# Sparse weights times rows as seven block products per pair of chunks

## What is computed

```python
inter = xf @ c1_w.T @ c2_w.T                      # scores, 1792 per row
blk = inter.reshape(B * T, n_blocks, SPARSITY)    # 56 blocks of 32
idx = argmax(blk, axis=-1) + arange(0, 1792, 32)  # one winner a block
h = relu(einsum('bkm,bm->bk', w1[idx], xf))
out = einsum('bk,bkm->bm', h, w2t[idx])
x = layernorm(x + out)
```

## Time and profile before

| what | us |
|---|---|
| median of three runs (733.7 to 734.46) | 734.05 |
| profiled execution, its span | 731.9 |
| TensorE busy in it | 722.7 |
| VectorE busy | 480.2 |
| ScalarE busy | 214.3 |
| GpSimd busy | 157.1 |

### The profile page before, as it was taken

One profiled execution on the slowest core, in us unless ns is written; L12 is line 12 of the kernel. 1 busy time (PEld: TensorE's weight loads), 2 busy tenths in 40 slices (PEclk: granted clock), 3 DMA queues, 4 the chain that ended last, 5 costly groups with the idle time before them and its releaser, 6 DMA issues.

```text
span 731.9 us, 8884 instructions
## 1 busy us (share of the span) xinstructions
PE 722.7 (99%) x3457; PEld 334.0 (46%) x3457; DVE 480.2 (66%) x930; ACT 214.3 (29%) x341; POOL 157.1 (21%) x131
## 2 busy tenths in 40 slices
PE   8999999999999999999999999999999999999996
PEld 3444444444444444444444444444444444445444
DVE  5978897796877779677767779653755361125136
ACT  1575457435612212122122112122212221122130
POOL 0452443111111111111111111222212212222130
PEclk9999999999999999999999999999999999999999
DMA  9537319310000010100001334104020015001001
GB/s 326 248 124 206 58 15 379 67 48 11 1 17 18 20 20 9 25 20 20 5 19 20 79 81 92 23 4 101 16 75 7 1 29 133 1 0 58 1 1 57
DMA packets 40569, 44.57 MB, mean 61 GB/s; under 512 B 25040, under 2 KB 32848, under 8 KB 39632
## 3 DMA queue, kind: packets, MB, share of 16 engines
q1 hardware_dynamic: 37552, 39.29, 17.9%
q0 software_dynamic: 2112, 4.19, 3.4%
q10 hardware_dynamic: 864, 0.53, 0.2%
HBM read 34.33 MB, written 4.42 MB: 53 GB/s over the span
## 4 chain that ended last, share of the span: by engine, by line
PE 86%; issue 1%; POOL 1%; DVE 0%; ACT 0%
PE acc L469 31%; PE pb L449 24%; PE pa L449 24%; PE acc L775 2%; PE acc L546 2%; PE pick_b L612 1%; PE pick_a L612 1%; POOL big L998 1%; PE pick_a L597 0%; PE pick_b L775 0%; PE acc L465 0%; PE pick_b L465 0%; ACT work L836 0%; ACT work L820 0%; ACT pick_b L821 0%
## 5 line engine op out<-in xcount | busy, mean ns | idle before, releaser
L469 PE MATMUL acc<-big,work 128*128 128x512 f16 x1038 | 234.3, 379 | 0.0
L991 POOL TENSOR_TENSOR work<-work 128x512 f16<-128x512 f32 x92 | 110.2, 1201 | 479.9 <-ACT work L909 270.0
L449 PE MATMUL pa<-xs,big 128*128 128x512 f16 x816 | 188.8, 379 | 0.0
L449 PE MATMUL pb<-xs,big 128*128 128x512 f16 x816 | 187.2, 379 | 0.0
L469 PEld LDWEIGHTS acc<-big,work 128*128 128x128 f16 x1038 | 101.5, 98 | 121.0
L449 PEld LDWEIGHTS pa<-xs,big 128*128 128x128 f16 x816 | 78.6, 98 | 91.8
L449 PEld LDWEIGHTS pb<-xs,big 128*128 128x128 f16 x816 | 78.5, 98 | 91.6
L964 ACT ACTIVATE work<-work 128x512 f16<-128x512 f32 x52 | 32.6, 627 | 203.1 <-DVE work L1611 203.1
L546 PE MATMUL acc<-big 128*128 128x512 f16 x336 | 73.9, 379 | 0.3 <-DVE big L1228 0.2
L1611 DVE SCALAR_TENSOR_TENSOR work<-big,const_sb,pa 128x512 f32<-128x512 f16 x28 | 20.8, 744 | 74.0 <-PE pa L449 67.4
L909 ACT ACTIVATE work<-work 128x512 f16<-128x512 f32 x40 | 25.2, 630 | 143.8 <-DVE work L1365 143.8
(11 more groups left out here) (176 smaller groups left out, 548.8 us busy)
## 6 DMA issues: line engine op xcount, KB each, us to landing
big<-in_w_all SPq DMA_DIRECT2D x2, 3840.0 KB, 17.2
big<-spread_rows SPq DMA_DIRECT2D x16, 448.0 KB, 9.1
big<-in_x_t SPq DMA_DIRECT2D x16, 256.0 KB, 8.7
rows<-in_x POOLq DMA_DIRECT2D x4, 1024.0 KB, 11.8
big<-in_w_all SPq DMA_DIRECT2D x2, 1536.0 KB, 11.2
out<-rows SPq DMA_DIRECT2D x3, 1024.0 KB, 4.3
big<-in_w_all SPq DMA_DIRECT2D x1, 2048.0 KB, 14.4
big<-in_w_all SPq DMA_DIRECT2D x2, 1024.0 KB, 11.6
```

Source lines behind the costliest of these rows:

```text
L449: mm = nc.tensor.matmul(dst[:, :], weights(wp)(kc * P, P), x_part16(g, xp, kc), start=(kc == 0 and wp == xp), stop=(kc == KC - 1 and wp == 1))
L469: mm = nc.tensor.matmul(acc[t][:, :], act_part(pair, j, ap, t * P, P), weights(wp)(0, H), start=(first and ap == wp), stop=(last and ap == 1))
L991: nc.gpsimd.tensor_tensor(act_part(pair, j, 1), act32[j], act_part(pair, j, 0), ALU.subtract).then_inc(act_lo, 1)
```

## The change

For each pair of chunks the hidden product (256 columns of weights by 512 rows, inner length 512) is cut in 2 x 2 blocks, and the eight block products are replaced by seven of sums of blocks (Strassen's identity in the form with shared sums). A block is 128 weight columns by 256 rows with inner length 256: 2 slices x 3 matmuls of 256 columns.

- `raise_quad` on GpSimd makes four sums in float32 (`quad`, 1024 columns) from two high-low pairs, `sums_high` on ScalarE makes the high part of them, `lower_quad` on GpSimd the low part. There are 15 such jobs: one for each of the seven units' weights, two for each group's rows. Five run in phase 1 (pairs 11, 12, 17, 18, 19), ten in the sparse phase, in the units 0 to 5, 8, 9, 15 and 16.
- `seven_products` on TensorE writes P1, then P5 and P7, then P2 and P6 (on P1), then P3 and P4, in halves of `pa` and `pb`. ScalarE copies P1, P5 and P7, and P1 + P6 to SBUF (`take_products`). VectorE adds two parts, of 256 and 512 columns, in `mask_hidden`, GpSimd two of 256 columns in `add_products`. The mask then reads `act32` instead of the PSUM banks.
- Spread loads go out in two parts for each group, 8 and 6 chunks.
- The order of the last second products is changed, one exponent of the scales is lower (`TOP2`), and the scratch for dynamic DMAs is 4096 bytes instead of the default.

```diff
+SUM_JOBS = (("w", 0), ("w", 1), ("x", 0, 0), ("x", 0, 1), ("w", 2), ("w", 3), ("w", 4), ("w", 5), ("w", 6),
+            ("x", 1, 0), ("x", 1, 1), ("x", 2, 0), ("x", 2, 1), ("x", 3, 0), ("x", 3, 1))
+JOB_IN_SWIGLU = {11: 0, 12: 1, 17: 2, 18: 3, 19: 4}
+JOB_IN_SPARSE = {0: 5, 1: 6, 2: 7, 3: 8, 4: 9, 5: 10, 8: 11, 9: 12, 15: 13, 16: 14}
...
+            def block_product(dst, weights, moving, first=False):
+                for k in range(KH):
+                    for wp, xp in ((0, 0), (0, 1), (1, 0)):
+                        mm = nc.tensor.matmul(dst, weights(k, wp), moving(k, xp), start=(first and k == 0 and wp == xp), ...
+            def seven_products(g, u, between=None, after_first=None):
...
+                if n:
+                    pe.wait_ge(c11_ready, n)
+                block_product(pa[:, low_half], w_block(0, 0), x_block(0, 0), True).then_inc(p1_ready, 1)
+                if n:
+                    pe.wait_ge(c12_ready, n)
+                else:
+                    pe.wait_ge(swiglu_ready, N1)
+                if u == 0:
+                    pe.wait_ge(sums_lo, SUM_JOBS.index(("x", g, 1)) + 1)
+                if g == 0:
+                    pe.wait_ge(sums_lo, SUM_JOBS.index(("w", u)) + 1)
+                block_product(pb[:, low_half], w_sum(SLOT_S1), x_sum(SLOT_T1), True)
+                block_product(pb[:, high_half], w_sum(SLOT_S3), x_sum(SLOT_T3)).then_inc(p57_ready, 1)
...
+                pe.wait_ge(p1_taken, n + 1)
+                block_product(pa[:, high_half], w_block(0, 1), x_block(1, 0))
+                block_product(pa[:, low_half], w_sum(SLOT_S2), x_sum(SLOT_T2)).then_inc(p26_ready, 1)
...
+                pe.wait_ge(p57_taken, n + 1)
+                block_product(pb[:, low_half], w_sum(SLOT_S4), x_block(1, 1))
+                block_product(pb[:, high_half], w_block(1, 1), x_sum(SLOT_T4)).then_inc(p34_ready, 1)
...
+            unit2(3, 4, none, none, none, "none")
+            for t in range(2):
+                second_tile(3, t, acc[t][:, :])
+            unit2(3, 5, none, none, none, "none")
+            second_tile(3, 2, acc[2][:, :])
+            for h, bank in enumerate(last_halves):
+                second_tile(3, TPG - 1, bank, h * HALF, HALF)
+            unit2(3, 6, none, none, none, "none")
+            for t in range(2):
+                for u in (4, 5):
+                    second_tile(u, t, acc[t][:, :])
+            for t in range(2):
+                second_tile(6, t, acc[t][:, :], done=True)
             for u in (4, 5, 6):
-                unit2(3, u, none, none, none, "none")
...
+                second_tile(u, 2, acc[2][:, :], done=(u == U2 - 1))
             for h, bank in enumerate(last_halves):
-                for u in (3, 4, 5, 6):
+                for u in (4, 5, 6):
```

ScalarE, with `sums_high` behind the relus of its unit:

```diff
+            def take_products(n):
+                act.wait_ge(p1_ready, n + 1)
+                if n:
+                    act.wait_ge(c11_ready, n)
+                act.activation(p1_kept, pa[:, 0:HT], ACT.Copy).then_inc(p1_taken, 1)
+                act.wait_ge(p57_ready, n + 1)
...
+                act.activation(p57_kept, pb[:, :], ACT.Copy).then_inc(p57_taken, 1)
+                act.wait_ge(p26_ready, n + 1)
...
+                act.activation(q_kept, pa[:, 0:HT], ACT.Copy).then_inc(q_taken, 1)
...
+            def hidden(g, u, high=None, late=False, early=None):
+                take_products(g * U2 + u)
...
+                if g * U2 + u in JOB_IN_SPARSE:
+                    sums_high(JOB_IN_SPARSE[g * U2 + u])
```

GpSimd:

```diff
+                for h, (hi, lo) in enumerate(pairs):
+                    step(nc.gpsimd.tensor_tensor(quad[:, h * 2 * BLK:(h + 1) * 2 * BLK], hi, lo, ALU.add))
+                settle()
+                if kind == "w":
+                    step(nc.gpsimd.tensor_tensor(blocks[3], blocks[2], blocks[3], ALU.add))
+                    settle()
+                    step(nc.gpsimd.tensor_tensor(blocks[2], blocks[0], blocks[2], ALU.subtract))
+                    settle()
+                    step(nc.gpsimd.tensor_tensor(blocks[0], blocks[3], blocks[0], ALU.subtract))
+                    settle()
+                    nc.gpsimd.tensor_tensor(blocks[1], blocks[1], blocks[0], ALU.subtract).then_inc(quad_ready, 1)
...
+            def lower_quad(i):
...
+                pool.wait_ge(sums_hi, i + 1)
...
+                nc.gpsimd.tensor_tensor(lo, quad[:, :], hi, ALU.subtract).then_inc(sums_lo, 1)
+            def add_products(n):
+                pool.wait_ge(p57_taken, n + 1)
...
+                step(nc.gpsimd.tensor_tensor(p57_sum, p57_kept[:, 0:HT], p57_kept[:, HT:2 * HT], ALU.add))
+                settle()
+                pool.wait_ge(q_taken, n + 1)
+                pool.wait_ge(act_lo, N1 + 2 * n)
+                nc.gpsimd.tensor_tensor(act32[1][:, HT:GT], p57_sum, q_kept, ALU.add).then_inc(c22_ready, 1)
...
+            for n in range(GROUPS * U2):
+                g, u = n // U2, n % U2
+                add_products(n)
+                if n in JOB_IN_SPARSE:
+                    raise_quad(JOB_IN_SPARSE[n])
                 for j in range(2):
...
+                        low(GROUPS * U1 + n, j, m)
+                if n in JOB_IN_SPARSE:
+                    lower_quad(JOB_IN_SPARSE[n])
```

VectorE:

```diff
             def mask_hidden(g, u):
+                n = g * U2 + u
+                dve.wait_ge(q_taken, n + 1)
+                dve.wait_ge(act_lo, N1 + 2 * n)
+                v.tensor_tensor(act32[0][:, 0:HT], pa[:, HT:GT], p1_kept, ALU.add).then_inc(c11_ready, 1)
+                dve.wait_ge(p34_ready, n + 1)
+                v.tensor_tensor(work32[:, HT:3 * HT].rearrange("p (a t) -> p a t", a=2), pb[:, :].rearrange("p (a t) -> p a t", a=2),
+                                q_kept.unsqueeze(1).broadcast_to([P, 2, HT]), ALU.add).then_inc(c12_ready, 1)
...
                 for j in range(2):
+                    if j:
+                        dve.wait_ge(c22_ready, n + 1)
-                    v.scalar_tensor_tensor(out=act32[j], in0=spread(g, u * 2 + j), scalar=own_rank, in1=(pa, pb)[j][:, :],
+                    v.scalar_tensor_tensor(out=act32[j], in0=spread(g, u * 2 + j), scalar=own_rank, in1=act32[j],
                                            op0=ALU.is_equal, op1=ALU.mult).then_inc(masked, 1)
```

More of the change, by code:

```diff
@@ L72 @@
 X1_SCALE = 2.0 ** 9
+TOP2 = 12
 HID_SCALE = 2.0 ** -17
@@ L251, in program @@
         spread_out = sem("spread_out")
-        spread_in = [sem(f"spread_in{g}") for g in range(GROUPS)]
+        spread_in = [[sem(f"spread_in{g}_{h}") for h in range(2)] for g in range(GROUPS)]
         winner_ready, winner_turned, z_turned = sem("winner_ready"), sem("winner_turned"), sem("z_turned")
@@ L697, in second2 @@
                         after_first()
-            def hidden(dst, c, g, between):
-                split_product(dst, lambda part: w2_part(c, 0, part), g, between).then_inc(hid_ready, 1)
-            def unit2(g, u, after_first, after_hidden, after_third, kind, start=False, between=None):
[L706 to L713, removed]
+            def block_product(dst, weights, moving, first=False):
+                for k in range(KH):
+                    for wp, xp in ((0, 0), (0, 1), (1, 0)):
+                        mm = nc.tensor.matmul(dst, weights(k, wp), moving(k, xp), start=(first and k == 0 and wp == xp), skip_group_check=True,
+                                              stop=(k == KH - 1 and wp == 1))
+                return mm
@@ L1013, in _ @@
             add_rows(GROUPS - 1)
[L1014 to L1021 removed]
+            steps = Steps(pool, pool_step)
@@ new lines, in _ @@
+            for u in range(1, GROUPS * U1):
+                low(u, 0, u * 2)
+                if u in JOB_IN_SWIGLU:
+                    raise_quad(JOB_IN_SWIGLU[u])
+                    lower_quad(JOB_IN_SWIGLU[u])
+                low(u, 1, u * 2 + 1)
+            for n in range(GROUPS * U2):
[3 more added lines that the diff above has]
+                    raise_quad(JOB_IN_SPARSE[n])
+                for j in range(2):
+                    m = N1 + n * 2 + j
+                    if g == GROUPS - 1 and u >= LATE:
+                        pool.wait_ge(act_hi, m + 1)
+                        nc.gpsimd.tensor_tensor(late_part(u, j, 1), act32[j], late_part(u, j, 0), ALU.subtract).then_inc(act_lo, 1)
+                    else:
+                        low(GROUPS * U1 + n, j, m)
+                if n in JOB_IN_SPARSE:
+                    lower_quad(JOB_IN_SPARSE[n])
```

174 lines of the change are left out of this document (135 added, 39 removed).

## The result

The changed kernel takes 754.74 us (median; 754.48 to 757.25), the one before 733.88 on the same chip: 1.0291 times as long, 95% interval 1.0272 to 1.0310, 20.9 us slower. The prediction was 738 with a range of 727 to 745: the direction was right, the size far off.

The account below looks back on a forecast made before the run. PE was taken to bound the kernel. Span 731.9 - 16.7 (products) + 3.4 (tail) + 11.2 + 3.2 + 3.3 (waits on PE) + 0.3 (dense phase) = 736.6, as a run 738.7, given as 738; range 727 to 745.

Parts of the forecast that it names:

- the saving: On PE, seven block products take 4.58 us instead of 5.18, 0.60 less; 28 pairs give 16.7 us, nearly certain.
- The tail: At the end, reordered second products let DVE end 6.9 us after PE, before 3.5: cost 3.4 us.
- the price of the port: In the sparse phase GpSimd loses 0.9 us a unit to masks, 0.5 to others; its cycle of 10.95 becomes 12.35.
- the 3.2 and 3.3 forecast for groups 1 and 2: Waits on PE from pairs of jobs at units 8, 9 (3.2 us) and 15, 16 (3.3 us).
- GpSimd's queue in group 0: Units 0 to 5: GpSimd's sums fall behind and ACT's P1 copy waits for them, 11.2 us of waits on PE.
- Costs set to nothing: Sums in the dense phase 0.3 us; spread loads, scores, DMA scratch and added DVE work nothing.
- margin of 0.4: Scores: z to its landed transpose takes 3.5 us of 3.9, hidden by 0.4; up to 0.5 a tile if DVE is late.
- The third: Rival: DVE late as well, picks wait for `lower_quad`, z and scores slip; 6 to 10 us more, 746; chance 0.13.
- the second rival: No stalls at all, if GpSimd's sums take half as long or ACT is freed sooner: 720.8; chance 0.07.
- its own bound without a loss from the port: Stalls in units 0 to 5, 8, 9 and 15, 16: 3.1 + 0.7 + 0.8 = 4.6 us.
- the first rival: GpSimd keeps up, its port losses fall into its own waits; 5 to 6 us of stalls remain, 726; chance 0.3.

Follow-up runs that it names:

- e1: The changed kernel with four row sums moved from units 8, 9, 15, 16 to 11, 12, 18, 19: 744.19 us, 1.0151.
- e3: The kernel before, plus GpSimd instructions of ten sums in units 0 to 5, 8, 9, 15, 16, results unread: 744.34 us, 1.0148.
- e6: e3 with the ten sums moved to units 0, 2 to 6, 11, 12, 18, 19, so nearly none meets a normalisation: 737.18 us, 1.0048.
- e5: e1 with ACT's copy of the raised sums behind its copy of the next P1: 741.87 us, 1.0120.
- e2: The changed kernel without the sparse phase's ten block sums, reusing earlier sums (values not the reference's): 727.44 us, 0.9915.
- e4: The changed kernel with 70 unread 512-column matmuls put ahead of PE's seven longest waits: 752.80 us, 1.0271.

## Why the prediction was off

**What bounds the kernel, and the saving: right.** 28 x 0.60 came as forecast, by the pace of units without a wait (9.76 for 10.36 us).

**The tail: right,** 2.9 for 3.4.

**The failed step is the price of the port.** The prediction said that "one waits for the other's whole instruction", and then charged it to GpSimd: 0.9 a unit for masks and "0.5 a unit for picks, normalisation and x1_low", all as a delay of GpSimd's cycle. It counted what GpSimd loses and not what DVE loses. What it charged was right: beside the two masks at 449.95 GpSimd's operations of 256 columns take 1.26 and 1.06 us instead of 0.72. But a DVE instruction of 0.16 us can lose 0.9, more than those two masks together (1.89 for 1.42 us), and the normalisation is ten of them and two of 512 columns in a row: 5.0 us in the trace of after. DVE's idle third, to which the added work was sent at no cost, does not cover that, since c11 is queued behind it. Two experiments show the size: moving four sums away from it gives back 10.5 us (e1), and in the old kernel it makes 6.8 of 10.7 us (e3 against e6). By stretches, the 3.2 and 3.3 forecast for groups 1 and 2 measured 9.3 and 8.6; with the meeting gone (e1), 2.4 and 3.4.

**GpSimd's queue in group 0: the mechanism is there, at half the size.** The stretch of units 1 to 5 lost 14.9 us for 11.2. The waits for ACT in it are of the kind that was forecast, but they are 5.5 us (1.53, 1.11 and 2.88); 3.34 are the wait for c11, 1.0 are waits for scores (0.35 and 0.66), and the 5.0 left are, by estimate, matmuls at the lower clock. That the stretch without the c11 wait, 11.6, comes near 11.2 is luck. ACT's order, which the prediction took for the cause, explains at most 2.3 us in all (e5). In e5's profiled execution, which lies 2.2 above its median, group 0 is no shorter than in e1 (78.9 and 77.6 us from P1 of unit 0 to that of unit 6), since what is freed is lost to the scores and c11.

**Costs set to nothing.** The dense phase's five sums cost 1.9 instead of 0.3: four waits of 0.43 to 0.49 for transposes whose values DVE finishes late (three ahead of score products, one ahead of z). Unit 0 costs 2.8: 1.76 for the bank (e2 shows it without any sum in the sparse phase), 0.73 for scores whose margin of 0.4 was too thin. Together 4.4 us that the sum lacked. It had no term for the clock either: some 13.7 us of slower matmuls in the profiled execution, of which e4 gives back 1.9 by the medians and 5.3 between the two profiled executions.

**Instruction sizes.** GpSimd's 256-column operation, of which the earlier trace rows had no example, has a median of 0.724 us, where a straight line gave 0.63; 1024 columns take 2.13 (2.2 assumed); ACT's copy of 256 columns 0.36 to 0.38 (0.47). Lines 1207 and 1200, min, median and max in ns:

```profile
L1207 POOL TENSOR_TENSOR big<-big x28: 718/724/1172, 432.4 to 729.3; 128x256 f32<-128x256 f32 x28
...
L1200 POOL TENSOR_TENSOR big<-quad,big x13: 2119/2126/2285, 392.2 to 634.3; 128x1024 f16<-128x1024 f32 x13
```

**Rivals.** The third (DVE late as well, 746) had the right place and half the price, by the wrong operation: it looked at the picks. The first two fail by size: the first needed all stalls under 13.3 us, and 40.4 less the tail are 37.5. The prediction also says that without the port the sum is the second rival's; its own bound without a loss from the port, 4.6 us of stalls, is near the first rival instead. The rule that the prediction cited from the Trainium skill (GPSIMD Engine Reference, Specifications), that GpSimd's SBUF interfaces contend with VectorE's instructions of two SBUF inputs, held in after (a `tensor_tensor` of two SBUF inputs on 4 columns, L1615, 1.08 us at 459.24 for 0.16); on how many instructions it falls was missed. e3's 1.06 and 1.08 are `tensor_scalar` instructions with one input tensor, of which the prediction's sentence says nothing.

What stays open: how group 0's loss divides between the queue, the masks and the clock. No run of the seven products has group 0's sums without the masks in SBUF, or without the sum that meets the normalisation. The old kernel with the sums (e3), whose masks read PSUM, waits 4.3 us in group 0 (3.17 and 1.12).

## What to carry to other kernels

Before work is moved to GpSimd, look at what VectorE does at that moment, and count instructions, not columns: in a chain of tiny operations between SBUF tiles, each that begins beside a GpSimd instruction can wait until that one ends. Where both must be, keep them apart in time; that alone was worth 10.5 of 20.9 us here, for one line changed. And a saving on the engine that bounds the kernel shortens every margin of the others, so a margin of some tenths of a microsecond should be forecast as a loss, not as nothing.

## What the runs showed of the hardware

- A 4-column VectorE instruction between SBUF tiles takes 0.16 us alone and 0.57 to 1.08 beside GpSimd's of 0.72 to 1.16 (after and e3), and a `tensor_scalar` with one input tensor is hit as well (0.17 became 1.06); the pick's product of 448 columns went from 0.39 to 2.24 beside one of 1024. Instructions with an input in PSUM (0.62 for the pick's first two steps), the pick's `tensor_reduce` from SBUF (0.62) and those that make statistics (2.46 for four) kept their times.
- The two engines alternate instruction by instruction: in a gap of 0.08 us between two of GpSimd's, one of VectorE's of 0.16 runs, and the next is blocked again.
- GpSimd is held up as well: its operation of 256 columns took 1.26 and 1.06 us beside two masks, 0.72 alone.
- From 465 to 475 us, behind an idle time of 3.34, TensorE's granted clock had means of 0.69 and 0.63, with 12 narrow matmuls in 2.52 us instead of 1.47; keeping it at 1.00 by filled waits (e4) gave 1.9 us of 754.7.
